# Channel attention of a four-layer kernel: extremes kept in SBUF and taken over both tiles at once, a fourth PSUM staging bank

## The reference

```
q, k, v = 1x1 convolutions of the normed x         # k, v padded by 3 on each side
kwin[c, pixel, (i, j)] = k window 7x7, + rel_h[c, i] (channels 0-127) or + rel_w[c, j] (128-255)
attn = softmax(q[..., None] * kwin, axis=-1)       # per channel and pixel, over 49 taps
out  = sum(attn * vwin, axis=-1)
```

## Time and profile before

| | us |
|---|---|
| median of 3 runs (lowest, highest) | 9316.44 (9316.26, 9318.12) |
| the profiled execution's own time | 9307.04 |
| span of its trace, first to last instruction | 9305.5 |
| taps of the channel attention, first to last | 4056.4 to 8204.4 |

### The profile page before, as it was taken

The page is one execution under the profiler, slowest core; times in us unless marked ns, Lnnn a source line. Parts: engine busy times, 40 slices in busy tenths (PEclk is TensorE's granted clock), DMA queues, the critical chain, the costliest instruction groups (busy, mean ns, idle before and its releaser), DMA issues. The chain is left out here.

```text
span 9305.5 us, 159969 instructions
## 1 busy us (share of the span) xinstructions
PE 8011.6 (86%) x55850; PEld 6805.6 (73%) x55850; DVE 5823.2 (63%) x9258; ACT 3539.4 (38%) x6969; POOL 4537.8 (49%) x2070
## 2 busy tenths in 40 slices
PE   3888886759996777569999999999999999938999
PEld 2666664649996565458888888888888888836777
DVE  3555555454442343479888989888888889842110
ACT  3444444313332222234445545444445545530000
POOL 2444443003332000047778878777777878831111
PEclk9999998879998888889999999999999999969999
DMA  5111113846775455410000000000000000052111
GB/s 195 52 52 61 53 52 129 295 143 144 146 146 142 173 160 149 159 70 17 6 17 17 17 17 17 17 13 17 6 17 17 17 17 17 8 164 105 63 61 55
DMA packets 435343, 703.76 MB, mean 76 GB/s; under 512 B 273645, under 2 KB 280301, under 8 KB 425390
## 3 DMA queue, kind: packets, MB, share of 16 engines
q1 hardware_dynamic: 389550, 502.28, 17.4%
q0 software_dynamic: 38656, 176.79, 6.3%
q10 hardware_dynamic: 6528, 16.78, 0.6%
HBM read 422.53 MB, written 273.22 MB: 75 GB/s over the span
## 5 line engine op out<-in xcount | busy, mean ns | idle before, releaser
L1705 POOL TENSOR_TENSOR e_ev<-e_se,e_v 128x2048 f32<-128x2048 f32 (+1 forms) x896 | 3311.6, 3714 | 916.6 <-ACT e_se L1671 916.6
L1671 ACT ACTIVATE e_se<-e_stage 128x512 f32<-128x512 f32 x3136 | 1878.2, 599 | 2082.4 <-PE e_stage L1545 2056.3
L1795 DVE SCALAR_TENSOR_TENSOR e_stage<-e_k,e_rl,e_qp 128x512 f32<-128x512 f32 x3136 | 2302.6, 746 | 318.6 <-ACT e_se L1671 279.2
L1552 PE MATMUL e_pv_sum<-e_ident,e_ev 128*128 128x128 f32 x12544 | 1874.1, 273 | 38.1 <-issue 37.6
L1552 PE MATMUL e_pe_sum<-e_ident,e_se 128*128 128x128 f32 x12544 | 1878.0, 272 | 0.1
L1552 PEld LDWEIGHTS e_pe_sum<-e_ident,e_se 128*128 128x128 f32 x12544 | 1556.3, 139 | 227.3 <-issue 2.0
L1552 PEld LDWEIGHTS e_pv_sum<-e_ident,e_ev 128*128 128x128 f32 x12544 | 1487.9, 141 | 264.8 <-issue 211.4
L1545 PE MATMUL e_stage<-e_top,e_minus 128*128 128x512 f32 x3136 | 1508.7, 481 | 45.3 <-DVE e_stage L1795 43.9
L363 POOL TENSOR_TENSOR a_pr<-a_pr,a_rden 128x480 f32<-128x480 f32 x512 | 493.9, 985 | 683.0 <-DVE a_rden L583 683.0
L852 POOL DMA_DIRECT2D agg<-c_ot x384 | 329.0, 862 | 950.9 <-DVE c_ot L910 839.1
L886 PE MATMUL c_pa<-c_x_high,c_w_high 128*128 128x320 f32 x1920 | 602.3, 314 | 111.4 <-DVE c_w_low L965 111.4
(11 more groups left out here) (154 smaller groups left out, 12357.7 us busy)
## 6 DMA issues: line engine op xcount, KB each, us to landing
xn<-n_xnp POOLq DMA_DIRECT2D x32, 2450.0 KB, 14.9
qkv<-b_ot SPq DMA_DIRECT2D x120, 512.0 KB, 5.8
c_xt<-qkv SPq DMA_DIRECT2D x384, 160.0 KB, 4.3
agg<-c_ot POOLq DMA_DIRECT2D x384, 160.0 KB, 3.0
n_xt<-x SPq DMA_DIRECT2D x24, 2048.0 KB, 11.8
a_xb<-xn SPq DMA_DIRECT2D x32, 840.0 KB, 6.2
e_xb<-xn SPq DMA_DIRECT2D x16, 1540.0 KB, 7.0
f_xb<-xn SPq DMA_DIRECT2D x32, 700.0 KB, 6.0
```

Source lines behind the costliest of these rows:

```text
L1552: last = nc.tensor.matmul(acc[:, c * PART:(c + 1) * PART], lhsT=src[:, c * PART:(c + 1) * PART], rhs=ident[:], is_transpose=True, start=j ...
L1671: nc.scalar.activation(se[(t * K2 + o) % NSE][:, i], stage[:, bank_of(t, j), :], ACT.Exp)\
L1705: nc.gpsimd.tensor_tensor(split(ev[(t * NG2 + g) % NEV][:, 0:size]), split(se[(t * K2 + o) % NSE][:, i:i + size]), window(v[h], h, u, o, i ...
L1795: nc.vector.scalar_tensor_tensor(rows(stage[:, bank_of(t, j), :]), win, rl[:, h, o:o + 1], rows(qp[:]), ALU.add, ALU.mult).then_inc(multip ...
```

## The change

Three things:

1. The extreme steps work on both tiles of a half-band at once: 17 steps of 1024 elements instead of 34 of 512 (NEXT_ is now 17, spread over the same taps, the last after tap 43 of the second tile). Their running value is not in a PSUM bank but in SBUF: the max chain builds up in `high`, the min chain in a new tile `ext` of 1024 elements. PE's first subtraction of a half-band waits for all 17.
2. The bank that is free now becomes a fourth bank of `stage` (NST = 4): DVE's tap waits for the exponential of four taps back. The rules for odd cases (bank_lag) go, since 4 divides 196 taps. Q_AT moves from tap 46 to 45.
3. `od` goes: the division writes into `es`, the transposes read it there, and the copy of the next sums waits for the transposes before.

```
-        NSE, NEV, NST = 4, 4, 3
+        NSE, NEV, NST = 4, 4, 4
+        ext = sb("ext", [PART, BPX])
-        od = sb("od", [PART, TPX])
-        ext = pb("ext", [PART, TPX])
...
-        NEXT_ = 2 * sum(CHAIN)
-        TOP_AT = [2 * CHAIN[0] + (w + 1) * CHAIN[1] for w in range(2)]
+        NEXT_ = sum(CHAIN)
...
-            g = t * NTAP + j
-            return 1 if g == TPB * NTAP - 1 else g % NST
-        def bank_lag(t, j):
-            return 2 if t * NTAP + j in (1, TPB * NTAP - 1) else NST
+            return (t * NTAP + j) % NST
...
-                if j == 0:
-                    pe.wait_ge(ext_step, halves(n, t // 2, NEXT_, TOP_AT[u]))
+                if u == 0 and j == 0:
+                    pe.wait_ge(ext_step, halves(n, t // 2, NEXT_, NEXT_))
...
             def take_e_sums(n, t):
                 act.wait_ge(e_summed, tiles(n, t, NTAP, NTAP))
-                if t > 0 or not isinstance(n, int):
-                    act.wait_ge(inverted, tiles(n, t, NINV, 0))
+                if not isinstance(n, int) or n * TPB + t > 0:
+                    act.wait_ge(turned_back, tiles(n, t, 1, 0))
                 nc.scalar.activation(es[:], pe_sum[:], ACT.Copy).then_inc(e_taken, 1)
...
-                i = int(s >= 2 * CHAIN[0])
+                i, o = divmod(s, CHAIN[0]) if s < 2 * CHAIN[0] else (1, CHAIN[0])
...
-                of_tile = slice(w * TPX, (w + 1) * TPX)
+                to = (high, ext)[i]
                 if o < K2:
-                    win = one_window(near[i], w * RT * PW + (o * PW if h % 2 == 0 else o))
+                    win = one_window(near[i], o * PW if h % 2 == 0 else o, R2)
                     if o == 0:
-                        nc.vector.tensor_scalar(rows(ext[:]), win, r[:, o:o + 1], None, ALU.add).then_inc(ext_step, 1)
+                        nc.vector.tensor_scalar(rows(to[:]), win, r[:, o:o + 1], None, ALU.add).then_inc(ext_step, 1)
                     else:
-                        nc.vector.scalar_tensor_tensor(rows(ext[:]), win, r[:, o:o + 1], rows(ext[:]), ALU.add, op)\
+                        nc.vector.scalar_tensor_tensor(rows(to[:]), win, r[:, o:o + 1], rows(to[:]), ALU.add, op)\
                             .then_inc(ext_step, 1)
...
-                    nc.vector.tensor_tensor(to, q[h % 2][:, of_tile], ext[:], ALU.mult).then_inc(ext_step, 1)
+                    nc.vector.tensor_tensor(to[:], q[h % 2][:], to[:], ALU.mult).then_inc(ext_step, 1)
                 else:
-                    nc.vector.tensor_tensor(top[h % 2][:, of_tile], high[:, of_tile], ext[:], ALU.max).then_inc(ext_step, 1)
+                    nc.vector.tensor_tensor(top[h % 2][:], high[:], ext[:], ALU.max).then_inc(ext_step, 1)
...
-                nc.vector.tensor_tensor(od[:], pv_sum[:], rs[:], ALU.mult).then_inc(divided, 1)
+                nc.vector.tensor_tensor(es[:], pv_sum[:], rs[:], ALU.mult).then_inc(divided, 1)
```

More of the change, by code:

```diff
@@ L1401, in window, with one_window @@
             return bass.AP(tensor=a.tensor, offset=a.offset, ap=[a.ap[0], [step, taps], [PW, RT], [1, WW]])
-        def one_window(t, first):
+        def one_window(t, first, high_=RT):
             a = t[:, first:first + 1]
-            return bass.AP(tensor=a.tensor, offset=a.offset, ap=[a.ap[0], [PW, RT], [1, WW]])
+            return bass.AP(tensor=a.tensor, offset=a.offset, ap=[a.ap[0], [PW, high_], [1, WW]])
         def rows(t):
@@ L1585, in back @@
                 for c in range(NBLK2):
-                    last = nc.tensor.transpose(pj[:, c * PART:(c + 1) * PART], od[:, c * PART:(c + 1) * PART], ident[:])
+                    last = nc.tensor.transpose(pj[:, c * PART:(c + 1) * PART], es[:, c * PART:(c + 1) * PART], ident[:])
                 last.then_inc(turned_back, 1)
@@ L1760, in extreme_step @@
                     dve.wait_ge(ext_step, halves(n, h, NEXT_, s))
-                i = int(s >= 2 * CHAIN[0])
+                i, o = divmod(s, CHAIN[0]) if s < 2 * CHAIN[0] else (1, CHAIN[0])
                 op = (ALU.max, ALU.min)[i]
                 r = rl[:, h % 2]
-                w, o = divmod(s - i * 2 * CHAIN[0], CHAIN[i])
-                of_tile = slice(w * TPX, (w + 1) * TPX)
+                to = (high, ext)[i]
                 if o < K2:
-                    win = one_window(near[i], w * RT * PW + (o * PW if h % 2 == 0 else o))
+                    win = one_window(near[i], o * PW if h % 2 == 0 else o, R2)
                     if o == 0:
-                        nc.vector.tensor_scalar(rows(ext[:]), win, r[:, o:o + 1], None, ALU.add).then_inc(ext_step, 1)
+                        nc.vector.tensor_scalar(rows(to[:]), win, r[:, o:o + 1], None, ALU.add).then_inc(ext_step, 1)
                     else:
-                        nc.vector.scalar_tensor_tensor(rows(ext[:]), win, r[:, o:o + 1], rows(ext[:]), ALU.add, op)\
+                        nc.vector.scalar_tensor_tensor(rows(to[:]), win, r[:, o:o + 1], rows(to[:]), ALU.add, op)\
                             .then_inc(ext_step, 1)
                 elif o == K2:
-                    if i == 0 and w == 0:
+                    if i == 0:
                         dve.wait_ge(proj_copied, halves(n, h, NPJ, NQUERIES))
-                    to = high[:, of_tile] if i == 0 else ext[:]
-                    nc.vector.tensor_tensor(to, q[h % 2][:, of_tile], ext[:], ALU.mult).then_inc(ext_step, 1)
+                    nc.vector.tensor_tensor(to[:], q[h % 2][:], to[:], ALU.mult).then_inc(ext_step, 1)
                 else:
-                    nc.vector.tensor_tensor(top[h % 2][:, of_tile], high[:, of_tile], ext[:], ALU.max).then_inc(ext_step, 1)
+                    nc.vector.tensor_tensor(top[h % 2][:], high[:], ext[:], ALU.max).then_inc(ext_step, 1)
             def multiply(n, t, j, first=False):
@@ L1787, in multiply @@
                     dve.wait_ge(query_placed, tiles(n, t, 1, 1))
-                lag = bank_lag(t, j) if not (first and t * NTAP + j == 1) else NST
-                if t * NTAP + j >= lag or not first:
-                    dve.wait_ge(exp_done, tiles(n, t, NTAP, j - lag + 1))
+                if t * NTAP + j >= NST or not first:
+                    dve.wait_ge(exp_done, tiles(n, t, NTAP, j - NST + 1))
                 elif t * NTAP + j == 0:
@@ L1807, in divide @@
                 dve.wait_ge(inverted, tiles(n, t, NINV, NINV))
-                if t > 0 or not isinstance(n, int):
-                    dve.wait_ge(turned_back, tiles(n, t, 1, 0))
-                nc.vector.tensor_tensor(od[:], pv_sum[:], rs[:], ALU.mult).then_inc(divided, 1)
+                nc.vector.tensor_tensor(es[:], pv_sum[:], rs[:], ALU.mult).then_inc(divided, 1)
             def add(n, t):
```

## The result

The changed kernel takes 9761.9 us in the median of 4 runs (9752.8 to 9779.8), the one before 9316.35 beside it: a ratio of 1.0483, 95% interval 1.0465 to 1.0501, slower by 446 us. The forecast was 9572 in a range of 9400 to 9790.

What follows compares the result with a forecast made beforehand. PE bound the loop at 96.8%, 129.7 us a half-band; DVE would need 112.5 + 22.1 + 3.5 = 138.1, +8.4 over 31 half-bands = +261, less 5.3 before the loop, +256: 9572 us, range 9400 to 9790.

Steps and rivals of the forecast that it cites:

- DVE's steps and POOL's product wait for each other as a whole: Channel attention loop: steps with SBUF operands and POOL's products each wait for the other's whole instruction; forecast's chance 0.72.
- Prices without disturbance: New 1024-element steps on DVE: scalar_tensor_tensor 1.28 us, tensor_tensor 1.225, tensor_scalar 0.75; 19.0 us a half-band after overlap.
- The wait of a step: Each of 17 extreme steps waits 1.3 us for POOL, 22.1 us a half-band on DVE.
- random arrival: Reading of a step's wait: steps meet POOL, busy 104.0 of about 138 us, at random; 1.42 us a step.
- reading (b): DVE and POOL in step: DVE returns after 2.51 us to a POOL instruction of 3.71; 1.20 us left to wait.
- Rivals A and B: A: waits disappear in DVE's slack, 9311 us, chance 0.09; B: no blocking, 9213 to 9283 us, chance 0.07.
- C's bound of 1.89 us a step: Rival: POOL is running whenever a step comes, so each waits 1.89 us; 9883 us, chance 0.12 for above 9790.
- of its waits those for the sums stay ... 3.5: Of DVE's waits in the loop only those for the copied sums remain: 109.1 / 31 = 3.5 us a half-band.
- POOL's slack covers its loss: POOL loses at most 20.5 us a half-band, covered by 25.7 us idle; busy total up by as much as 640 us.
- The granted clock, one of the prediction's signs of being wrong: Prediction is wrong if the clock, 1.00 in the loop before, falls because PE is less busy; no size given.
- The fourth bank and the query placing at nothing: Fourth staging bank's gain, at most 0.9 to 3.1 us a half-band, and earlier query's cost, up to 1.3, counted as nothing.
- on fewer instructions: Skill page's rule that each instruction pays a fixed cost; 17 fewer extreme steps save DVE 3.0 us a half-band before waits.

Runs made afterwards that it cites:

- x_one_input: Changed kernel with all 17 extreme steps made reductions over one element with a single SBUF input; 9298.7 us, ratio 0.9991 to the kernel before.
- x_512: Changed kernel with 34 extreme steps of 512 elements, operands still in SBUF, instead of 17 of 1024; 10473.4 us, ratio 1.1243 to the kernel before.
- x_short_pool: Changed kernel with POOL's products cut to 2, 2, 2 and 1 taps instead of 4 and 3; 9348.1 us, ratio 1.0039 to the kernel before.
- x_before_short_pool: Kernel before the change with POOL's products cut to 2, 2, 2 and 1 taps; 9317.1 us, ratio 1.0006 to the kernel before.
- x_moved: Changed kernel with its 17 steps at other taps, two more among taps 0 to 12 of the second tile; 9650.3 us, ratio 1.0358 to before.
- x_three_banks: Changed kernel with three staging banks and the query placed at tap 46 again; 9783.1 us, ratio 1.0508 to the kernel before.

## Why the prediction held, and where it fell short

- **DVE's steps and POOL's product wait for each other as a whole: right, and shown.** Taking away the second SBUF operand removes it (x_one_input), more meetings make it worse (x_512), shorter products shrink it (x_short_pool) and do nothing where there are no such steps (x_before_short_pool). The plain tensor_tensor, of which no row of before told, is held like the others: the one at e_high takes 3.67 us in the mean against 1.22. By that the trace agrees with the Trainium skill, page "SBUF — State Buffer", section Who interferes with whom.
- **Prices without disturbance: right** to 0.02 us each. For the tensor_scalar (0.75 forecast, 0.752 measured) the working shown doesn't give the number: 1418 ns for 2304 elements are 0.62 ns an element, which alone would make 0.63 us.
- **The wait of a step: right in size, in part by luck.** 1.3 was forecast and 1.23 measured, but neither random arrival nor reading (b) is what happens; the mean comes out of 17 nearly fixed waits between 0 and 3.4 us. The longest step, forecast at 5.5 us, lasts 4.69. Rivals A and B did not occur. C's bound of 1.89 us a step was not reached.
- **The step that was mis-sized: "of its waits those for the sums stay ... 3.5".** The prediction's 129.7 is a mean over all 32 half-bands; the 31 with steps went from 130.3 to 144.8 us, +14.5 where +8.4 was forecast, and the missing 6.1 x 31 = 189 us are the whole miss of 190 (9572 against 9762). By the shares above, DVE's need grew from 116.1 (0.891 x 130.3) to 132.3 us (0.914 x 144.8), +16.2 where 112.5 + 22.1 - 115.5 = +19.1 was forecast. Its idle time fell from 14.2 to 12.5 us, by 1.7, where it was to fall to 3.5, by 10.7. So the idle time is 9.0 us too few in the forecast, and the need 2.9 too many. The waits for the sums are as forecast (90.5 us in the rows after, 3.0 a half-band); what the forecast put at nothing is the wait for a free bank (157.4 us, 5.1 a half-band), for PE's weighted sum before the division (55.2, 1.8) and for the query (35.9, 1.2).

Why does DVE still wait for banks when it sets the pace? A half-band is not one sum. By the starts of the taps, in the mean of 24 half-bands of each trace (us; in brackets how long DVE had nothing under way):

| taps | before | after | x_moved |
|---|---|---|---|
| 0 to 33, first tile | 48.7 (3.3) | 48.8 (3.4) | 48.8 (3.4) |
| 34 to 48, first tile | 18.2 (1.2) | 21.7 (0.8) | 21.7 (0.8) |
| 0 to 12, second tile | 22.7 (6.6) | 22.4 (6.0) | 22.4 (1.6) |
| 13 to 48, second tile | 41.1 (3.2) | 52.4 (2.4) | 48.8 (2.7) |

The loss lies in the second and fourth rows, and most of DVE's idle time in the first and third. Behind the division, from the first step there to `top`, DVE had hardly any slack even before (the kernel before, then the kernel after, columns as above):

```profile
6095.85:6131.40 35.55, 35.55 (x291) 33.28 (x290) 35.06 (x55) 18.70 (x32) 33.71 (x10) 1.00 0.01 2
```

```profile
6017.91:6064.06 46.15, 39.98 (x291) 36.27 (x289) 46.15 (x42) 18.76 (x32) 38.32 (x10) 0.93 0.01 1
```

Before, PE was busy in all of the 35.55 us and DVE in 35.06. After it, DVE is busy in all of the 46.15 us and PE in 39.98. Thirty taps now take 46.15 us where 32 took 35.55, and the ten steps among them wait 14.5 us together (26.6 us of duration against 12.1 undisturbed). At the tile's start the opposite holds (kernel after, DVE; the last number is idle time):

```profile
6007.93 0.76 DVE L1785 SCALAR_TENSOR_TENSOR e_stage<-e_k,e_rl,e_qp 128x512 f32<-128x512 f32 x1 [1.14 <-ACT e_se L1664]
...
6012.34 0.75 DVE L1785 SCALAR_TENSOR_TENSOR e_stage<-e_k,e_rl,e_qp 128x512 f32<-128x512 f32 x1 [1.90 <-ACT e_se L1664]
6014.10 0.76 DVE L1785 SCALAR_TENSOR_TENSOR e_stage<-e_k,e_rl,e_qp 128x512 f32<-128x512 f32 x1 [1.01 <-ACT e_se L1664]
6016.65 0.69 DVE L1798 TENSOR_TENSOR e_es<-e_pv_sum,e_rs 128x512 f32<-128x512 f32 x1 [1.79 <-PE e_pv_sum L1545]
```

Here PE has the projections to do, and DVE idles 5.8 us in four waits. It can't use that time for what comes later: the ring holds four taps, and the division is a meeting point, since it needs PE's last weighted sum of the tile and PE's next one needs the division. Behind it DVE starts with no lead, and straight into a long wait, 2.5 of the 3.75 us of 6017.91. The average of 14.2 us of slack was real and in the wrong place. x_moved tested this: two more steps in the third row cost nothing there.

- **POOL's slack covers its loss: right.** Its busy time rose from 3327.8 us to 3693.3, 365 of the 640 allowed (kernel after, POOL's groups by form):

```profile
L1698 POOL TENSOR_TENSOR e_ev<-e_se,e_v 128x2048 f32<-128x2048 f32 x448 | 2044.2, 4563 | 922.5 <-ACT e_se L1664 918.5
L1698 POOL TENSOR_TENSOR e_ev<-e_se,e_v 128x1536 f32<-128x1536 f32 x448 | 1649.1, 3681 | 76.2 <-ACT e_se L1664 76.2
```

PE waited for no weighted product in the changed kernel, but for 22.3 us in x_short_pool.

- **The granted clock, one of the prediction's signs of being wrong, did fall,** from 1.00 to 0.98 in the loop and to 0.93 in the stretch shown above. It is a small part at most: if PE had bound the whole loop, 0.02 x 4597 = 92 us by estimate, and in the stretch of 0.93 DVE was busy all the time, so that a faster PE would have shortened nothing there. No run separates the rest.
- **The fourth bank and the query placing at nothing: right** within 21 us of the median and 41 of the taps, by x_three_banks. ACT's wait at the query rose from 12.3 to 69.4 us, and DVE's for it from 15.4 to 35.9.
- **The Trainium skill's page "VectorE: DVE Perf Modes", Rules for kernel authors, on fewer instructions:** its gain is there in DVE's time once nothing blocks, 20.7 us a half-band for the 17 steps of x_one_input against 25.1 for the 34 before. In the whole it bought 3 us, because DVE had slack already; in the changed kernel the steps take 41.5.

Open: why the stages in front, unchanged, end up to 44 us apart in these traces. One execution of each kernel can't tell whether that goes with the kernel or with the execution; runs of one kernel alone lie up to 44 us apart (x_short_pool, 9320.0 to 9364.0). Open too is the exact rhythm, which decides whether a given step waits 0 or 3.4 us. It repeats from half-band to half-band, and was not worked out ahead.

## What to carry to other kernels

Before moving a VectorE operand from PSUM to SBUF beside a busy GpSimd, look for one pair of such instructions anywhere in the trace and compare maximum with median: a wait of this kind hides in durations. If the operand has to move, few long instructions on VectorE and short ones on GpSimd were the better choice here (9762 against 10473 us, and 9348 against 9762). And compare an added wait with the slack of the stretch in which it falls, between two points where the engines must meet, not with an average over the period.

## What the hardware showed unexpectedly

- The granted clock of PE was lower where PE had more gaps: 1.00 in the loop before, 0.98 after, 0.92 in x_512, where PE is busy 2517.45 of 3000 us. In one slice (kernel after):

```profile
6040.00:6050.00 10.00, 7.47 (x47) 6.68 (x46) 10.00 (x10) 3.02 (x6) 6.15 (x3) 0.83 0.00 1
```

PE was busy 7.47 of these 10 us, and the clock of 0.83 means that it ran for a third of them at 1.2 GHz instead of 2.4. Before it fell PE had been busy for 0.97 of the 3.50 us from 6040.00, while DVE's step of 6037.69 waited 3.4 us. In the next 10 us the clock was 1.00 again.

- POOL loses less than DVE holds: its products grew by 365 us in all, while DVE's steps worked for 31 x 20.5 = 636 us. The rest must have fallen into POOL's idle time, as the step of 6027.16 did; how much did was not counted.
